# A two layer transformer on one core: attention scores in one pass from 12 bit parts, maxima 12 heads ahead, one bias on ScalarE

## The chip, the cores and the metric

The kernel runs on one core of a Trainium2 chip. The time is that of one launch on the device, in microseconds. Three runs of the kernel before took 324.24 to 324.75 us, median 324.54 us.

## The reference

Two post-norm layers over x of 8 batches, 256 tokens, width 128, all float32. The layer outputs go through residual sums and a layer norm after attention and after the feed-forward part. What matters here:

```python
# layer 0: attention with 16 heads of 8, then a feed-forward part with butterflies
qkv = x @ Wqkv + bqkv                          # q, k, v per head, d = 8
scores = einsum('bqhd,bkhd->bhqk', q, k) / sqrt(8)
out = einsum('bhqk,bkhd->bqhd', softmax(scores), v) @ Wproj + bproj
h = x @ W_exp + b_exp                          # 128 -> 512
h = gelu(butterfly(h, up_weights) + up_bias)   # linear, 9 stages of pairs
y = butterfly(h, down_weights) @ W_con + b_con + down_bias
# layer 1: low rank q, k, v, rotated q and k, 4 key heads repeated, causal mask
q = rope(x @ Wqa @ Wqb);  k, v = split(x @ Wkva @ Wkvb);  k = rope(k)
out = einsum('bhqk,bkhd->bqhd', softmax(causal(q k^T / sqrt(8))), v) @ Wout + bout
y = (silu(x @ w_gate^T) * (x @ w_up^T)) @ w_down^T     # 128 -> 384 -> 128
```

## The kernel before, in words

**Steps.** All the work is one loop over `STEPS`: g runs over the 256 heads (two layers x 8 batches x 16 heads) by `QUAD` = 4, and each engine walks the same loop with its own instructions in a hand-written order, tied by semaphores. I call the steps of a batch by g modulo 16: 0, 4, 8 and 12. An offset such as `AT_ROPE` = -36 says in which step, counted from a batch's first head, a task of that batch is done. `batch_at`, `tile_at`, `half_at`, `attention_at`, `projected_at` turn g into the batch, the 512-token tile or the half batch whose turn it is. Layer 1 begins at g = 128.

**Scores.** A head has only 8 features, so four heads share TensorE: `QK` holds each head of a group in a strip of 32 partitions, and four matmuls of different strips run beside each other. Every head's scores are made twice. `max_scores` (L382) makes them with queries on the partitions, for the row maxima, `LEAD` = 16 heads ahead of `exp_scores` (L395), which makes them with keys on the partitions, for the exponential. In the second, row 31 (`MAXROW`) of each strip holds ones against the negative row maximum, so that the subtraction comes with the product. All of it is float32. `scores` (L405) issues two heads' maxima and two heads' exponential scores in turn, twice a step, over all eight PSUM banks; the bank of a head is free again when VectorE has taken its maximum or ScalarE its exponential (`take`, L360).

**The way of a maximum.** VectorE's `maximum` (L778) writes one column of `mx` per head: a reduction in layer 0 (L789), a masked add and minimum in layer 1 (L797). After 8 heads TensorE turns `mx` (`turn_maxima`, L446, two transposes of 128 columns into 8 rows), ScalarE copies the 8 rows (`copy_maxima`, L653), and SyncE's queue moves them into the `MAXROW` rows (`maxima`, L306). This is done in steps 8 and 0 (`AT_MT`), 8 heads ahead of the use.

**The way of q and k.** TensorE projects (`project`, L455), ScalarE copies (`copy_projection`, L659), in layer 1 GpSimd rotates (L1041 to L1043, in step 12), and SyncE's queue spreads the result over `QK`, a ring of four batches (`spread`, L312).

**The rest of a step,** behind the scores on TensorE: projections, products with V (L585), transposes, and the feed-forward matmuls (L531 and L600 in layer 0, L541 and L552 in layer 1). GpSimd does the causal cut of the exponentials (L986), the layer norms (`normalise`, L938) and the preparation of layer 0's butterflies (`paths`, `mix`). VectorE adds the bias of layer 0's way up (L842); ScalarE's table for the gelu (L726) must be loaded before it and the exponential's again after it.

## Time and profile before

| | |
|---|---|
| median of the runs | 324.54 us |
| the profiled execution, its own time | 324.64 us |
| span of its instructions | 322.8 us |
| TensorE busy | 298.1 us, 92% |
| VectorE busy | 246.8 us, 76% |
| ScalarE busy | 181.5 us, 56% |
| GpSimd busy | 177.4 us, 55% |
| granted TensorE clock, mean | 0.991 |

Between the span and the execution's own time lie 1.8 us. The profile gives, per engine, busy time over the span; then groups of instructions by source line with their total and mean time; then who waited for whom. PE is TensorE, PEld its weight loads, DVE VectorE, ACT ScalarE, POOL GpSimd. A float32 matmul stands in the trace as two records, each with its own weight load. A busy share is a mean over 64 steps that have different limits, so single steps are read as well: the first exponential of each step on ScalarE marks where a step begins.

### The profile page before, as it was taken

What the parts mean: (1) busy time and instruction counts of PE and PEld (TensorE: products, weight loads), DVE (VectorE), ACT (ScalarE), POOL (GpSimd) and SP (SyncE); (2) the same over time, 40 slices, a digit from 0 to 9 for tenths busy, and PEclk for the clock granted to TensorE, in tenths of its full rate; (3) what the DMA queues carried; (4) which work ended last, traced back from release to release, by engine and by line L of the source; (5) the groups of instructions that cost most, each with busy time, mean ns of one, the idle gap of its engine ahead of it and who ended that gap; (6) DMA issues with size and microseconds to landing.
All of it is one profiled execution on the core that took longest, in us unless ns stands there. A gap on an engine that the chain in (4) does not pass through costs nothing.

```text
span 322.8 us, 10410 instructions
## 1 busy us (share of the span) xinstructions
PE 298.1 (92%) x3770; PEld 218.9 (68%) x3770; DVE 246.8 (76%) x943; ACT 181.5 (56%) x396; POOL 177.4 (55%) x296
## 2 busy tenths in 40 slices
PE   8789979999999999989999899999999999999763
PEld 4566666676677765866677657776787777767553
DVE  4887686779868697677958788597998999945555
ACT  2455665666775749456675638466555464644110
POOL 6498082321215217176266988398877746477332
PEclk9999999999999999999999999999999999999978
DMA  7743252011000110301103030301112110000000
GB/s 231 247 144 68 43 133 60 1 36 35 4 4 1 38 36 2 66 3 38 35 4 66 5 65 4 69 4 37 36 34 55 28 29 1 20 3 20 16 18 32
DMA packets 9470, 14.29 MB, mean 44 GB/s; under 512 B 2140, under 2 KB 5196, under 8 KB 9292
## 3 DMA queue, kind: packets, MB, share of 16 engines
q1 hardware_dynamic: 8988, 13.09, 16.8%
q8 instruction: 31, 0.51, 0.7%
q10 hardware_dynamic: 432, 0.53, 0.5%
q14 instruction: 19, 0.16, 0.2%
HBM read 6.28 MB, written 1.05 MB: 23 GB/s over the span
## 4 chain that ended last, share of the span: by engine, by line
PE 68%; DVE 19%; issue 6%; ACT 4%; POOL 1%; POOLq 0%; DVEq 0%; ACTq 0%
PE bank L391 17%; PE bank L585 15%; DVE mx L789 7%; PE bank L400 7%; PE bank L541 5%; PE bank L600 4%; PE bank L467 4%; PE bank L552 3%; PE bank L531 3%; DVE masked_s L797 2%; PE bank L452 2%; PE bank L563 1%; ACT E L700 1%; DVE hid L813 1%; PE bank L482 1%
## 5 line engine op out<-in xcount | busy, mean ns | idle before, releaser
L700 ACT ACTIVATE E<-bank 128x512 f32<-128x512 f32 (+1 forms) x256 | 119.3, 547 | 96.2 <-PE bank L400 95.2
L391 PE MATMUL bank<-QK 31*128 31x256 f32 (+1 forms) x1024 | 115.7, 364 | 10.1 <-DVE mx L789 4.2
L400 PE MATMUL bank<-QK 32*128 32x256 f32 (+1 forms) x1024 | 114.3, 366 | 0.9 <-ACT E L700 0.9
L391 PEld LDWEIGHTS bank<-QK 31*128 31x128 f32 x1024 | 88.3, 184 | 30.8 <-issue 11.6
L789 DVE TENSOR_REDUCE mx<-bank 128x2 f32<-128x512 f32 x128 | 79.2, 683 | 14.8 <-PE bank L391 14.7
L400 PEld LDWEIGHTS bank<-QK 32*128 32x128 f32 x1024 | 85.2, 184 | 2.7 <-ACT E L700 1.5
L797 DVE CUSTOM_DVE_ANT_0 masked_s<-bank,mask_sb 128x256 f32<-128x256 f32 (+1 forms) x256 | 73.2, 351 | 3.8 <-PE bank L391 3.5
L585 PE MATMUL bank<-E,V 128*32 128x256 f32 (+1 forms) x1024 | 55.1, 355 | 0.6 <-DVE mx L789 0.4
L986 POOL TENSOR_SCALAR_AFFINE_SELECT E<-E 128x512 f32<-128x512 f32 x64 | 39.2, 640 | 16.5 <-ACT E L700 16.5
L585 PEld LDWEIGHTS bank<-E,V 128*32 128x32 f32 x1024 | 29.3, 109 | 20.3 <-issue 2.1
L993 POOL TENSOR_TENSOR at<-turned,rec 128x256 f32<-128x256 f32 x16 | 10.1, 631 | 46.8 <-DVE rec L894 46.8
L872 DVE STREAM_TRANSPOSE turned<-bank 128x256 f32<-128x256 f32 x32 | 14.4, 450 | 22.6 <-PE bank L585 22.6
L541 PE MATMUL bank<-xt,wf 128*128 128x256 f32 x96 | 25.8, 412 | 0.2 <-DVE hid L813 0.2
L939 POOL TENSOR_SCALAR nm_a<-mv_a 128x2 f32<-128x2 f32 x15 | 2.9, 195 | 36.5 <-DVE mv_a L759 36.5
L541 PEld LDWEIGHTS bank<-xt,wf 128*128 128x128 f32 x96 | 18.3, 202 | 5.3 <-ACT E L700 2.5
L797 DVE DVE_READ_ACCUMULATOR2_ANT mx<- 128x1 f32 x256 | 21.1, 82 | 0.0
L600 PE MATMUL bank<-down,hid 128*128 128x128 f32 x128 | 16.1, 279 | 0.2 <-DVE mx L797 0.2
L600 PEld LDWEIGHTS bank<-down,hid 128*128 128x128 f32 x128 | 14.9, 192 | 1.9 <-ACT E L700 1.2
L811 DVE SCALAR_TENSOR_TENSOR gated<-th,bank 128x256 f32<-128x256 f32 x24 | 10.0, 418 | 7.8 <-ACT th L719 7.5
L719 ACT ACTIVATE th<-bank 128x256 f32<-128x256 f32 x24 | 9.3, 389 | 10.4 <-PE bank L541 9.1
L531 PE MATMUL bank<-xt,wup 128*128 128x512 f32 x32 | 15.1, 596 | 0.0
L942 POOL TENSOR_SCALAR ln_a<-r_a,nm_a,rstd_a 128x128 f32<-128x128 f32 x30 | 13.3, 452 | 1.6
(113 smaller groups left out, 400.1 us busy)
## 6 DMA issues: line engine op xcount, KB each, us to landing
QK<-qk SPq DMA_DIRECT2D x60, 64.0 KB
rs<-ry SPq DMA_DIRECT2D x16, 128.0 KB, 2.9
xb<-x_nat SPq DMA_DIRECT2D x1, 1024.0 KB, 5.0
xt<-x_t SPq DMA_DIRECT2D x1, 896.0 KB, 7.0
out<-ln_g SPq DMA_DIRECT2D x7, 128.0 KB, 1.9
wi<-wi_all SPq DMA_DIRECT2D x1, 576.0 KB, 5.1
QK<-mt SPq DMA_DIRECT2D x32, 8.0 KB
fac<-fac_u SPq DMA_DIRECT2D x1, 508.0 KB, 6.3
```

Of the source, the lines that this page charges most:

```text
L391: ins = nc.tensor.matmul(g_bank["max", m][:, cols], q, QK[rows, b % QK_RING, r, 1, keys], start=True, stop=True)
L400: ins = nc.tensor.matmul(g_bank["exp", m][:, c * T:(c + 1) * T - q0], QK[rows, b % QK_RING, r, 1, c * P:(c + 1) * P], QK[rows, b % QK_RING ...
L531: nc.tensor.matmul(bank[:, :], wup[:, c * P:(c + 1) * P], xt[:, n * FT:(n + 1) * FT], start=True, stop=True).then_inc(F0["up_ps"], 1)
L541: ins = nc.tensor.matmul(bank[:, s * T:(s + 1) * T], wf[:, s, c * P:(c + 1) * P], xt[:, i * T:(i + 1) * T], start=True, stop=True)
L585: ins = nc.tensor.matmul(bank[VCOL * j:VCOL * (j + 1), q0:T], values, E[:, (2 * n + e) % E_RING, j, k * T:(k + 1) * T - q0], start=(e == 0 ...
L600: ins = nc.tensor.matmul(bank[:, i * W:(i + 1) * W], hid0[:, c, s * P:(s + 1) * P], down[:, c, :], start=(c == 0), stop=(c == HC - 1))
L700: act.activation(E[:, a % E_RING, j, 0:n], g_bank["exp", m][:, 0:n], ACT.Exp, scale=SCALE)\
L789: ins = nc.vector.tensor_reduce(mx[:, n % 2, :, i], bank[:, :].rearrange("p (q k) -> p q k", q=QT), AX.X, ALU.max, negate=True)
L797: ins = nc.vector.tensor_tensor_reduce(out=masked_s[:, at % 2, lo:hi], in0=bank[:, lo:hi], in1=mask_sb[:, T + lo - hi:T], scale=-1.0, scal ...
L872: nc.vector.transpose(turned[:, t, :], g_bank["pv", n][:, 0:T]).then_inc(A["turned"], 1)
L942: ins = nc.gpsimd.tensor_scalar(N["ln"][:, parity, s, :], N["r"][:, s, :], N["nm"][:, s:s + 1], N["rstd"][:, s:s + 1], ALU.add, ALU.mult)
L986: nc.gpsimd.affine_select(out=e, in_=e, pattern=[[0, 4], [1, P]], compare_op=ALU.is_ge, fill=0.0, base=0, channel_multiplier=-1).then_inc( ...
```

## The change

**Parts.** q and k are each split into a high part with 12 bits of mantissa and a low part, the rest. `QK` gets the type float32r, in which a matmul is one instruction where float32 takes two. A strip of 32 rows now holds, for each of the 8 features, four products: with the rows filled by parts as high/high, high/low, low/high and low/low, one matmul over the strip sums them. The row maxima are split in the same way. Batch 0 keeps float32 (`whole`).

**More steps on the way.** ScalarE makes the high part (`high_parts`), GpSimd the low one (`low_parts`), the queue spreads both with six DMAs in place of four into `spread_qk`, and a cast to float32r writes `QK`, now a ring of two batches: by GpSimd in layer 0, by ScalarE in layer 1. The moves of `mt` and of the ones are gone.

**Maxima.** All rows of a strip are used up, so the maximum is subtracted by a matmul of its own: `less_maximum` adds ones times the two parts of the maximum into the same bank. GpSimd splits the maxima (`part_maxima`), TensorE turns them with four float32r matmuls into 128 rows, ScalarE copies 128x512 in place of 8x256. `LEAD` is 12 in place of 16, and the turning is in steps 12 and 4, four heads ahead of the use.

**Other.** ScalarE in place of VectorE adds the bias of layer 0's way up. Some tiles share room. GpSimd's `paths(0)` stands ahead of its loop with the first `part_maxima` behind it; the fetch of `xb`'s bias and the butterfly work of GpSimd are cut into smaller pieces over more steps. TensorE's start makes 12 maxima and not 16 before the loop.

The constants, and the tiles:

```diff
-ROWS, MAXROW = D, STRIP - 1
-QK_RING, V_RING, E_RING, LN_RING, BANKS = 4, 3, 4, 3, 8
+PARTS, SPREADS = 2, 6
+QK_RING, V_RING, E_RING, LN_RING, BANKS = 2, 3, 4, 3, 8
-QUAD, LEAD, AHEAD = 4, 16, 8
-AT_MT, HURRY = (-8, 0), BATCHES - 2
-AT_QK, AT_QKIN, AT_ROPE = (-44, -36), -28, -36
+QUAD, LEAD = 4, 12
+AT_MT, HURRY = (-4, 4), BATCHES - 2
+AT_QK, AT_QK1, AT_ROPE, AT_HIGH, AT_LOW, AT_SPREAD, AT_CAST = (-44, -36), -48, -36, -32, -32, -28, -16
...
-        QK = sb("QK", [P, QK_RING, GROUPS, 2, T])
+        spread_qk = sb("spread_qk", [P, GROUPS, 2, T])
+        QK = sb("QK", [P, QK_RING, GROUPS, 2, T], F32R)
+        mxp = sb("mxp", [P, 2, QT, 2, P], F32R)
+        ones_r = sb("ones_r", [P, P], F32R)
+        mt = sb("mt", [P, 2, 2, T], F32R)
```

SyncE's `spread`:

```diff
             def spread(b):
+                sp.wait_ge(A["low_ready"], b)
+                if b > 1:
+                    sp.wait_ge(A["qk_ready"], 2 * (b - 1))
+                for t in range(PARTS):
+                    sp.dma_start(spread_qk[3 * t:P:4, :, :, :], parts[:, b % 2, t, :, :]).then_inc(spread_in, 16)
+                for t in range(PARTS):
+                    for s in range(2):
+                        sp.dma_start(spread_qk[1 + t:P:4, :, s, :], parts[:, b % 2, (s + t) % 2, s, :]).then_inc(spread_in, 16)
```

TensorE: the new `less_maximum`, then in `scores` the waits and the order, then `turn_maxima`:

```diff
+            def less_maximum(m):
+                b, r, j = place(m)
+                rows = slice(STRIP * j, STRIP * (j + 1))
+                most = mt[rows, m // 8 % 2, r % 2, :]
+                if layer(b) == 0:
+                    ins = nc.tensor.matmul(g_bank["exp", m][:, :].rearrange("p (c t) -> p c t", c=2), ones_r[rows, :],
+                                           most.unsqueeze(1).broadcast_to([STRIP, 2, T]), start=False, stop=True)
+                else:
+                    for c in range(2):
+                        ins = nc.tensor.matmul(g_bank["exp", m][:, c * T:(c + 1) * T - c * P], ones_r[rows, :], most[:, c * P:T],
+                                               start=False, stop=(c == 1))
+                ins.then_inc(A["st_ps"], 1)
...
-                    elif b and m % H == 2:
-                        pe.wait_ge(qk_in[b % QK_RING], 16 * STRIPS * loads_of(b))
+                    elif b and m % 8 == 2:
+                        pe.wait_ge(A["qk_ready"], 2 * (b - 1) + m % H // 8 + 1)
...
-                        pe.wait_ge(m_in[n % 4], 16 * (n // 4 + 1))
+                        pe.wait_ge(A["mt_ready"], m // 8 + 1)
+                first = exps and exps[0] % QUAD == 2
                 for long in range(2):
+                    for m in exps if first else ():
+                        exp_scores(m, long)
                     for m in maxima:
                         max_scores(m, 1 - long)
-                    for m in exps:
+                    for m in () if first else exps:
                         exp_scores(m, long)
+                for m in exps:
+                    less_maximum(m)
...
-                pe.wait_ge(A["max_done"], 8 * (n + 1))
-                for q in range(QT):
-                    ins = nc.tensor.transpose(bank[0:8, q * P:(q + 1) * P], mx[:, n % 2, q, :], id32[:, :])
+                pe.wait_ge(A["mx_ready"], n + 1)
+                for r in range(2):
+                    for q in range(QT):
+                        ins = nc.tensor.matmul(bank[:, r * T + q * P:r * T + (q + 1) * P], mxp[:, n % 2, q, r, :], id_r[:, :], start=True, stop=True)
```

ScalarE: the copy of the maxima, `high_parts`; then in the loop the cast right after the four exponentials, the bias after the copies to `xt`, and the high parts after `copy_values`:

```diff
-                act.activation(mt[:, n % 2, :], g_bank["mt", n][0:8, 0:T], ACT.Copy).then_inc(A["mt_ready"], 1)
+                act.activation(mt[:, n % 2, :, :], g_bank["mt", n][:, :].rearrange("p (r t) -> p r t", r=2), ACT.Copy).then_inc(A["mt_ready"], 1)
...
+            def high_parts(b):
+                if layer(b) == 0:
+                    act.wait_ge(A["qk_out"], 2 * b)
+                else:
+                    act.wait_ge(A["rotated"], b - NB + 1)
+                if b > 2:
+                    act.wait_ge(A["qk_ready"], 2 * (b - 2))
+                act.activation(parts[:, b % 2, 0, :, :].bitcast(F32R), qk[:, :, :], ACT.Copy).then_inc(A["high_ready"], 1)
...
+                if (b := batch_at(g, AT_CAST, (1,))) is not None:
+                    act.wait_ge(spread_in, 16 * SPREADS * b)
+                    act.wait_ge(A["st_ps"], H * (b - QK_RING + 1))
+                    for half_batch in (slice(0, 2), slice(2, GROUPS)):
+                        act.activation(QK[:, b % QK_RING, half_batch, :, :], spread_qk[:, half_batch, :, :], ACT.Copy).then_inc(A["qk_ready"], 1)
...
+                        act.wait_ge(F0["up_ps"], HC * n + c + 1)
+                        act.activation(hid0[:, c, :], g_bank["up0", n, c][:, :], ACT.Identity, bias=bhid[:, c:c + 1]).then_inc(F0["pre_ready"], 1)
...
+                if (b := projected_at(g)) is not None and layer(b) == 0:
+                    high_parts(b)
+                if (b := batch_at(g, AT_HIGH, (1,))) is not None:
+                    high_parts(b)
```

VectorE loses:

```diff
-                        nc.vector.tensor_scalar(hid0[:, c, :], g_bank["up0", n, c][:, :], bhid[:, c:c + 1], None, ALU.add)\
-                            .then_inc(F0["pre_ready"], 1)
```

GpSimd: the new helpers, what stands ahead of the loop, the first tasks of a step, and its last:

```diff
+            def part_maxima(n):
+                pool.wait_ge(A["max_done"], 8 * (n + 1))
+                if n >= 2:
+                    pool.wait_ge(A["mt_ps"], n - 1)
+                found = mx[:, n % 2, :, :].rearrange("p q (r j) -> p q r j", r=2)
+                high, low = [mxp[:, n % 2, :, :, i:P:STRIP] for i in range(PARTS)]
+                link(nc.gpsimd.tensor_copy(high, found))
+                nc.gpsimd.tensor_tensor(low, found, high.bitcast(F32), ALU.subtract).then_inc(A["mx_ready"], 1)
+            def low_parts(b):
+                pool.wait_ge(A["high_ready"], b)
+                nc.gpsimd.tensor_tensor(parts[:, b % 2, 1, :, :], qk[:, :, :], parts[:, b % 2, 0, :, :], ALU.subtract)\
+                    .then_inc(A["low_ready"], 1)
+            low_parts(1)
+            pool.wait_ge(ld["up"], 32)
+            paths(0)
+            part_maxima(0)
             for g in STEPS:
+                if (n := half_at(g, AT_MT)):
+                    part_maxima(n)
+                if (b := batch_at(g, AT_CAST, (0,))) is not None and b:
+                    for half_batch in (slice(0, 2), slice(2, GROUPS)):
+                        nc.gpsimd.tensor_copy(QK[:, b % QK_RING, half_batch, :, :], spread_qk[:, half_batch, :, :]).then_inc(A["qk_ready"], 1)
...
+                if (b := batch_at(g, AT_LOW)) is not None and b > 1:
+                    low_parts(b)
```

## Rows read from the trace of the kernel before

**Rows 1.** The page: busy time (share of the span) and instructions.
```profile
PE 298.1 (92%) x3770; PEld 218.9 (68%) x3770; DVE 246.8 (76%) x943; ACT 181.5 (56%) x396; POOL 177.4 (55%) x296
```

**Rows 2.** Waits: who waited for what, us in total, times, longest.
```profile
ACT E L700 <- PE bank L400: 95.2, 60, 3.7
```

**Rows 3.** Busy time in stretches: steps 64 to 92, then steps 64, 76, 84, 92.
```profile
core 0: us, PE busy (x) PEld busy (x) DVE busy (x) ACT busy (x) POOL busy (x), PEclk, DMA share, GB/s
89.91:127.63 37.72, 37.18 (x472) 25.84 (x468) 29.41 (x65) 24.76 (x48) 14.74 (x25) 1.00 0.08 17
89.91:94.08 4.17, 4.17 (x60) 3.41 (x56) 1.77 (x7) 2.29 (x6) 0.38 (x1) 1.00 0.01 2
103.06:106.95 3.89, 3.89 (x48) 2.96 (x44) 2.49 (x5) 3.55 (x9) 1.97 (x5) 1.00 0.01 2
111.48:116.20 4.72, 4.72 (x44) 2.78 (x40) 4.29 (x8) 2.56 (x6) 2.36 (x3) 1.00 0.18 41
120.75:127.63 6.88, 6.53 (x106) 3.98 (x102) 5.36 (x12) 6.82 (x9) 5.73 (x8) 1.00 0.01 2
```

**Rows 4.** The same for layer 1: steps 144, 148 and 192, 196.
```profile
181.39:184.72 3.33, 2.36 (x44) 1.76 (x41) 2.31 (x17) 2.12 (x6) 3.25 (x3) 1.00 0.01 2
184.72:190.52 5.80, 5.80 (x80) 3.74 (x76) 4.60 (x21) 2.24 (x6) 4.69 (x8) 1.00 0.46 81
235.20:239.56 4.36, 4.36 (x58) 3.71 (x55) 4.16 (x23) 2.24 (x7) 3.16 (x7) 1.00 0.06 17
239.56:243.85 4.29, 4.29 (x78) 3.20 (x74) 3.32 (x22) 2.51 (x6) 3.15 (x7) 1.00 0.46 86
```

**Rows 5.** Timeline of PE: start us, us from first start to last end, instruction.
```profile
82.11 0.38 PE L391 MATMUL bank<-QK 31*128 31x256 f32 x2
82.33 0.38 PE L391 MATMUL bank<-QK 31*128 31x256 f32 x2
...
247.68 0.27 PE L391 MATMUL bank<-QK 31*128 31x128 f32 x2
...
247.79 0.28 PE L391 MATMUL bank<-QK 31*128 31x128 f32 x2
...
104.72 0.60 PE L522 MATMUL bank<-id,ln_f 128*128 128x128 f32 x4
```

**Rows 6.** Groups of ACT: line, instruction, count | busy us, mean ns.
```profile
L657 ACT ACTIVATE mt<-bank 8x256 f32<-8x256 f32 x32 | 11.4, 358 | 1.8 <-PE bank L452 1.8
L726 ACT ACTIVATE hid<-hid 128x2048 f32<-128x2048 f32 x4 | 7.6, 1910 | 0.0
L672 ACT ACTIVATE ry<-bank 128x512 f32<-128x512 f32 x8 | 4.8, 605 | 0.5 <-PE bank L467 0.2
```

**Rows 7.** Groups of POOL.
```profile
L1043 POOL TENSOR_TENSOR qk<-ry,rs 128x512 f32<-128x512 f32 x8 | 10.2, 1281 | 0.6
L977 POOL MEMSET QK<- 128x2048 f32 x3 | 5.3, 1806 | 0.0
L955 POOL TENSOR_TENSOR path<-fac 128x16 f32<-128x16 f32 x2 | 0.4, 219 | 5.6 <-DMA u_sb<-u 5.6
```

**Rows 8.** Groups of DVE.
```profile
L789 DVE TENSOR_REDUCE mx<-bank 128x2 f32<-128x512 f32 x128 | 79.2, 683 | 14.8 <-PE bank L391 14.7
L842 DVE TENSOR_SCALAR hid<-bank,bhid 128x512 f32<-128x512 f32 x16 | 11.8, 749 | 2.2 <-PE bank L531 1.8
```

**Rows 9.** Timeline of the first 24 us: POOL's paths, the first exponentials.
```profile
15.61 3.06 POOL L955 TENSOR_TENSOR path<-path,fac 128x32 f32<-128x32 f32 x5
...
20.09 2.28 ACT L700 ACTIVATE E<-bank 128x512 f32<-128x512 f32 x4 [1.42 <-PE bank L400]
```

**Rows 10.** Timeline of ACT in layer 1: four exponentials of a step, one tanh.
```profile
237.29 0.38 ACT L719 ACTIVATE th<-bank 128x256 f32<-128x256 f32 x1 [0.23 <-PE bank L541]
239.56 1.64 ACT L700 ACTIVATE E<-bank 128x384 f32<-128x384 f32 x4 [1.88 <-PE bank L400]
```

More of the change, by code:

```diff
@@ L183, in block_kernel, with part @@
         other = sb("other", [P, HC, W + 1])
-        facs = [sb(f"fac{i}", [P, HC, FAC]) for i in range(2)]
-        path = [sb(f"path{i}", [P, HC, FAC]) for i in range(2)]
+        room_a, room_c = sb("room_a", [P, 2 * GROUPS * T]), sb("room_c", [P, 4 * HC * FAC])
+        def part(room, first, shape):
+            size = int(np.prod(shape))
+            names = "abcd"[:len(shape)]
+            return room[:, first:first + size].rearrange(f"p ({' '.join(names)}) -> p {' '.join(names)}", **dict(zip(names, shape)))
+        facs = [part(room_c, i * HC * FAC, [HC, FAC]) for i in range(2)]
+        path = [part(room_c, (2 + i) * HC * FAC, [HC, FAC]) for i in range(2)]
         bfw_sb = sb("bfw_sb", [P, 2, 2, 2, HC])
@@ L390, in max_scores @@
                     cols, keys = (slice(T, T + P), slice(0, P)) if c == 0 else (slice(0, T), slice(0, T))
[L391 removed]
+                ins = nc.tensor.matmul(g_bank["max", m][:, cols], both[:, 0, c * P:(c + 1) * P], both[:, 1, keys], start=True, stop=True)
                 if c == 0:
```

213 lines of the change are left out of this document (95 added, 118 removed).

## The prediction

> **What bounds the kernel now.** I read the busy table first: TensorE is busy for 298.1 us, 92% of the span, and no other engine passes 76% [rows 1]. The waits agree: ScalarE's largest idle time, 95.2 us, ended with exponential scores from TensorE [rows 2]. Then I read single steps. From step 64 to 92, one 512-token tile of layer 0, the eight steps take 37.72 us, TensorE is busy in 37.18, VectorE in 29.41, ScalarE in 24.76, GpSimd in 14.74 [rows 3]. So TensorE bounds layer 0. Only step 92 stands apart: ScalarE is busy in 6.82 of 6.88 us there, by the gelu between two table loads. In layer 1 TensorE fills steps 148, 192 and 196, but VectorE has 4.16 of 4.36 us in step 192 [rows 4]. What TensorE gives up there, VectorE takes over after a few tenths of a us.
>
> **Scores, what goes.** Float32 records of one strip are 0.22 us apart for 256 columns and 0.11 us for 128, and a matmul is two records, so 0.43 us [rows 5]. A step of layer 0 has 16 matmuls on four strips: four rounds, 1.72 us.
>
> **Scores, what comes.** No float32r matmul is in this trace. One instruction of 256 columns is bounded below by the 0.11 us of a 128-column record, which pushes the same number of column passes (two for each column, if the four products of a float32 matmul are shared evenly by its two records), and above by the 0.22 us of one 256-column record. I take 0.11, since the second pass of such a record has no counterpart when one part is multiplied by one part. The added `less_maximum` is 512 columns for each head, and issue is in order: exponential and maximum scores for two rounds, `less_maximum` of two strips for two rounds, the first of them beside the exponential scores of the other two strips, and so on. I count seven rounds a step, 0.77 us (1.54 at the upper price). Saved: 0.95 us a step in layer 0. In layer 1 the rounds before are 768 columns of four passes, 1.3 us; after, the two short `less_maximum` matmuls of a head follow each other and I count about 1.0 us. Saved: 0.3 us.
>
> The Trainium skill, FP8 and Floating Point Precision, section TensorE Precision Notes, says that true FP32 is four passes and that a reduced mode reads 4 bytes and truncates to FP22. By it one pass of 256 columns is a quarter of 0.43 us, again 0.11; the trace agrees on the four passes only as far as two records of 0.22 us go.
>
> **The turn of the maxima.** Two transposes, 0.11 us apart like the four of L522 [rows 5], become four matmuls of 128 columns: +0.22 us on TensorE in steps 4 and 12. ScalarE's copy goes from 8x256 in 0.36 us to 128x512, as L672 in 0.60 us [rows 6]: +0.25 us. The matmul could cost up to 0.22 us each, as bound above.
>
> **ScalarE.** L672 and L726 (512 columns 0.60, 2048 columns 1.91 us) give 0.85 ns a column [rows 6]. Added are: the high part, 0.6 us a batch; the bias, 16 times about 0.6 us where VectorE took 0.75 [rows 8]; in layer 1 the cast, two of 1024 columns, 1.04 us each. In steps 64 to 92 this makes 24.76 + 4 x 0.25 + 2 x 0.6 + 4 x 0.6 = 29.4 us.
>
> **VectorE** loses 11.8 us of biases [rows 8], 3.0 in each of the four tiles: 29.41 becomes 26.4 in that stretch.
>
> **GpSimd.** Low part: 512 columns with two inputs, as L1043, 1.28 us a batch. Split of the maxima: two small operations as the 128x16 one of 0.22 us, with a wait between, 0.55 us twice a batch. The cast in layer 0, 2 x 1024 columns, lies between 0.9 us each (half a memset of 2048) and 2.6 (twice L1043); one input is nearer to the memset, I take 1.2 each [rows 7]. Layer 0: +4.8 us a batch on 7.4, no bound. Layer 1: +2.4 us.
>
> **The sum, layer 0.** No engine is near the old 37.7 us now, so I take for each step the latest of: TensorE's time less 0.95 (plus 0.22 in steps 4 and 12); ScalarE's with its additions; VectorE's; and the loop of four exponentials (2.29 us, step 64) and the scores behind them (0.7 to 0.8), 3.1 us. In the order of the tile: step 64 3.1 (was 4.17), then 3.5 and 4.0; step 76 3.5 (3.89; ScalarE's additions of 0.85 to its 3.55 partly sink into the lighter next step); 3.7; step 84 4.2 (4.72, two biases and a high part), 3.8; step 92 7.2, for the gelu's 6.82 remain and the larger copy of maxima joins. Sum 33.0, against 37.7: -4.7 us a tile. Two and a half such tiles from step 32 to 108 give -12 us; steps 4 to 28 have no gelu, less TensorE work and batch 0 in float32: -2. Together -14 us.
>
> **The start.** The first exponential runs at 20.09 us [rows 9]. Before it now stand 12 maxima and not 16, 4 x 0.62 us less (79.2 us over 128 [rows 8]), but the first split of the maxima stands behind GpSimd's `paths(0)`, whose end was at 15.3 us (its twin began at 15.61 [rows 9]); then split 0.55, turn 0.6, copy 0.6, scores 1.3: about 19. -1 us.
>
> **The sum, layer 1: a new chain.** This is where I expect a loss. Count from the first exponential of a step 0, S. ScalarE runs four exponentials, 1.64 [rows 10]; two casts, 2.08; the copy `ry`, moved here from step 4, 0.60; a tanh, 0.38 [rows 10]; the high part, 0.60: with gaps S + 5.5. GpSimd's last task of that step, `low_parts`, waits for it: S + 6.8. Queued behind that wait is step 4's `part_maxima`: S + 7.4. TensorE waits for it before `turn_maxima`, and behind that stands the rest of its step 4. That rest, for step 196, is 4.29 less 1.6 of scores with their drain less 0.86 of a projection that moves: 1.85 us [rows 4]. So the scores of step 8 end their first head at S + 7.4 + 0.5 + 1.85 + 0.6 = S + 10.35. Before, steps 192 and 196 took 4.36 + 4.29 = 8.65: +1.7. For steps 144 and 148 the rest is 5.80 - 2.46 = 3.3, the end S + 11.8 against 9.13: +2.7. The same sum over all seven such pairs (steps 112 to 208) gives +17 us. Given back: TensorE is shorter by 0.3 in each of steps 8 and 12, and VectorE and GpSimd use the pause to clear what they would have done in step 8: together I take 1.1 us a batch, 7.7 us. Net +9.5 us. From step 224 on no low part is left: -1 us.
>
> Total: 324.6 - 14 - 1 + 9.5 - 1 = 318 us, on the profiled execution's own time; the median is 0.1 us below it.
>
> **DMAs and other edits** I put at nothing. Two moves of the maxima and four of q and k become six, issued within one step; they are due 12 heads after their issue, three steps or 11 us. If that cover failed, the cast would wait and with it, in layer 1, ScalarE's exponentials. The maxima's 8 KB moves leave the path, and their slack of a step with them. Ring 2 in place of 4 asks only that the exponentials of batch b - 2 are issued; they are, a step earlier. Smaller pieces of `mix` lie beside TensorE.
>
> **Rivals.**
> A (forecast): as above, 311 to 324 us, chance 0.48.
> B: the chain does not bind, because ScalarE reaches the high part while TensorE is still in step 4's scores. For: ScalarE is busy in 2.24 of 4.36 us in step 192 [rows 4]. Against: its added 3.3 us fill just that. Time 318 - 9.5 = 308.5; range 303 to 311; 0.20.
> C: one float32r pass has the upper price, 0.22 us per 256 columns. Layer 0 then saves 0.18 us a step and loses 0.22 in two of four, nothing in sum; layer 1 pays 1900 columns, 1.6 us, for 1.3, 32 x 0.3 = +9. With the chain: 324.6 - 1 + 9.5 + 8 = about 341; 0.13. For: a transpose of 128 columns, a single record, is no faster than the two-pass records beside it (0.11 us, [rows 5]). Against: its weight load alone may set that.
> D, slower: GpSimd becomes the bound of layer 1. It has 3.2 us in each of steps 192 and 196 and over 4.6 in step 148 [rows 4]; with +2.4 us a batch it holds about 15.6 us of work in 16.9, and every wait of its queue (high part, variance, reciprocals) comes on top. It decides from the point where these waits pass 1.3 us a batch; at 3 us of them a batch takes 18.6, +1.7 us more than before for seven batches and hardly less for the pairs with layer norms of layer 0: +20 in layer 1 in place of +8.5, about 329; 0.17.
> That float32r does not run as one pass at all (0.43 us a round, seven rounds for four) would cost 1.3 us a step in layer 0 alone, over 360 us; 0.02.
>
> The Trainium skill, TensorE: Matmul & The Clock Gate, section LDWEIGHTS, gives a weight load as its columns over 1.2 GHz, 107 ns for 128 columns, and lets loads overlap only with matmuls of other row groups or into the background buffer. By it, if the load did not overlap its own strip, a round would be 0.21 us, C's price.
>
> **How the numbers follow.** 318 us is A's. The range, 303 to 334, takes in A, B and D with their bounds and leaves out C and the last, 15 in 100, and a little of the tails. This kernel's measurement can tell 0.2%, 0.65 us, from no change. Faster: 0.44 of A, all of B, a little of D: 0.65. Same 0.05. Slower 0.30.
>
> **What would show it.** Scores: the group of L391's successor with one record per matmul, 512 columns' `less_maximum` beside it, and rounds 0.11 us apart; 0.22 would be C. Layer 0: 33 us from step 64 to 92 and TensorE busy below 95%. Chain: in layer 1 TensorE's wait before `turn_maxima` in step 4 put down to GpSimd, 2 to 3 us, seven times, with `low_parts` just before; missing, it is B. GpSimd over 90% busy from step 128 on without a wait for ScalarE would be D. I am wrong if step 92's kind is longer than 7.5 us, for then ScalarE's additions do not sink anywhere.

## The result, and the profile after

The changed kernel takes 359.5 us (median of 4 executions, 355.0 to 363.8) against 324.6 us of the kernel before, run beside it on the same chip: ratio 1.094, interval 1.091 to 1.097. The forecast was 318 us, the range 303 to 334. It was wrong in sign and by 41.5 us. Medians are of all executions; ratios, and what is called a short mean below, take only those within 1.5% of a kernel's shortest, since the others had TensorE's lower clock for longer. The short mean of the changed kernel, over its four such executions here and in `after_again`, is 354.9 us.

The profiled execution of after is one of its longer ones (span 362.0 us; its shorter spans are 353.3 and 353.5), so stretches are read from it to find where time goes, and the ratio says how much.

The page of after, busy time, and the row of TensorE's granted clock in 40 slices (tenths of 2.4 GHz), first of before, then of after:

```profile
PEclk9999999999999999999999999999999999999978
```
```profile
PE 304.8 (84%) x3258; PEld 217.0 (60%) x3258; DVE 233.0 (64%) x927; ACT 223.4 (62%) x444; POOL 219.2 (61%) x391
...
PEclk9759996999999999969998699697699969899988
```

TensorE has 512 instructions fewer and yet more busy time than in [rows 1], and no engine is busy for the whole span. The clock row says half of why: before has the lower of the two clocks (1.2 in place of 2.4 GHz) for 5.8 us, all in its last 13 us; after has it for 71.6 us, in eleven stretches (its two shorter executions, by their mean granted clocks of 0.923 and 0.928, for 54 and 51 us). Matmuls in those stretches last up to twice as long. The waits say the other half (who waited for what; us in total, times, longest):

```profile
POOL parts L1026 <- ACT parts L697: 36.1, 10, 11.1
...
PE bank L467 <- POOL mxp L1021: 15.9, 10, 2.9
```

This is the chain that the prediction drew: GpSimd's `low_parts` (L1026) waits for ScalarE's high part (L697), and TensorE's turn of the maxima (L467) waits for GpSimd's split (L1021), ten times. Cut by the first exponentials of the steps, the 39 us between the two profiled spans lie as follows (us against before; combine is the last but two of the experiments):

| stretch | forecast | after | combine |
|---|---|---|---|
| up to the first exponential | -1 | +4.3 | -0.7 |
| steps 0 to 28 | -2 | +5.2 | +2.9 |
| steps 32 to 108 | -12 | -4.1 | -6.7 |
| steps 112 to 220, with all seven pairs of the chain | +9.5 | +30.7 | +0.8 |
| the rest | -1 | +3.1 | +0.8 |
| sum | -6.5 | +39.2 | -2.9 |

Some 7 us in the first two rows belong to this execution of after: in `swap_first`, which differs only in the order of two tasks on SyncE and whose start ran at the upper clock, they are -0.4 and +2.8. Layer 0 gave a third of its 12 us, and the stretch of the chain cost three times its 9.5. Steps 112 to 220 of before, after and combine:

```profile
145.37:268.39 123.02, 118.83 (x1625) 89.47 (x1622) 102.05 (x570) 73.35 (x166) 85.81 (x135) 1.00 0.16 33
...
150.77:304.52 153.75, 126.35 (x1416) 92.85 (x1412) 95.13 (x549) 98.72 (x195) 101.78 (x172) 0.87 0.19 62
...
140.88:264.70 123.82, 111.73 (x1416) 84.82 (x1408) 94.94 (x549) 97.77 (x194) 101.83 (x172) 0.97 0.24 76
```

The columns are those of [rows 3]: the span, then busy time of TensorE, its weight loads, VectorE, ScalarE and GpSimd. After and combine issue the same 1416 matmuls of TensorE there. Of the 29.9 us between them, 14.6 are the same matmuls taking longer (the lower clock has 41 us of this stretch in after, 7 in combine) and 15.3 are TensorE waiting.

Two steps of layer 1 and the tile of steps 64 to 92 of after, as [rows 3] and [rows 4] (busy us of each engine, granted clock):

```profile
core 0: us, PE busy (x) PEld busy (x) DVE busy (x) ACT busy (x) POOL busy (x), PEclk, DMA share, GB/s
195.34:199.99 4.65, 2.70 (x36) 2.07 (x35) 3.27 (x24) 4.65 (x9) 3.43 (x4) 1.00 0.01 4
...
199.99:209.68 9.69, 7.99 (x68) 4.21 (x64) 1.73 (x10) 3.64 (x9) 4.72 (x8) 0.65 0.38 127
...
109.61:114.32 4.71, 4.14 (x44) 3.30 (x46) 3.49 (x9) 4.54 (x10) 3.99 (x8) 1.00 0.00 0
...
126.50:133.87 7.37, 6.83 (x90) 4.30 (x94) 5.78 (x13) 7.31 (x10) 6.37 (x9) 1.00 0.03 7
97.49:133.87 36.38, 33.28 (x368) 22.18 (x368) 26.48 (x60) 28.86 (x53) 21.43 (x38) 1.00 0.20 67
```

Step 144 is full on ScalarE (4.65 of 4.65). Step 148 takes 9.69 us where [rows 4] has 5.80, at a mean clock of 0.65. The tile of layer 0 takes 36.38 us, not 33.0.

The timeline of step 148 in after shows both losses one after the other (start us, us, instruction, idle time before it and what ended it):

```profile
199.47 0.67 ACT L697 ACTIVATE parts<-qk 128x512 fp32r<-128x512 f32 x1
...
200.22 1.27 POOL L1026 TENSOR_TENSOR parts<-qk,parts 128x512 f32<-128x512 f32 x1 [1.37 <-ACT parts L697]
...
201.44 0.21 POOL L1020 CAST mxp<-mx 128x16 fp32r<-128x16 f32 x1
...
201.73 0.24 POOL L1021 TENSOR_TENSOR mxp<-mx,mxp 128x16 fp32r<-128x16 f32 x1
...
202.12 1.09 PE L467 MATMUL bank<-id_r,mxp 128*128 128x128 f32 x4 [1.68 <-POOL mxp L1021]
...
203.00 3.72 PE L545 MATMUL bank<-xt,wup 128*128 128x512 f32 x4
...
206.65 2.38 PE L599 MATMUL bank<-E,V 128*32 128x256 f32 x32
...
210.27 1.98 PE L545 MATMUL bank<-xt,wup 128*128 128x512 f32 x4
```

High part, low part, split, turn: TensorE waits 1.68 us. Then the same four matmuls of L545 that take 1.98 us in the next step at 2.4 GHz take 3.72 at 1.2. Here the clock costs more than the wait it came with: the clock fell at 201.7 us, inside the wait.

### The profile page after: what moved, and what is told of

Same layout as the page of the kernel before. It is cut to its first block, busy times and chain, and to the rows that moved or that the text cites. A ratio compares the mean times of both kernels' runs of the same rounds, so it can differ in the third digit from the quotient of the medians.

```text
span 362.0 us, 9594 instructions
## 1 busy us (share of the span) xinstructions
PE 304.8 (84%) x3258; PEld 217.0 (60%) x3258; DVE 233.0 (64%) x927; ACT 223.4 (62%) x444; POOL 219.2 (61%) x391
## 4 chain that ended last, share of the span: by engine, by line
PE 45%; POOL 27%; issue 11%; DVE 9%; ACT 3%; SPq 2%; DMA 1%; POOLq 0%; DVEq 0%; ACTq 0%
PE bank L599 11%; PE bank L545 4%; PE bank L467 4%; PE bank L387 4%; PE bank L555 4%; POOL parts L1026 3%; POOL E L1050 3%; PE bank L397 3%; PE bank L614 3%; POOL qk L1106 2%; PE bank L484 2%; POOL room_c L1104 2%; POOL room_c L1105 2%; DVE mx L832 2%; PE bank L566 2%
## 5 line engine op out<-in xcount | busy, mean ns | idle before, releaser
L840 DVE CUSTOM_DVE_ANT_0 room_c<-bank,mask_sb 128x256 f32<-128x256 f32 (+1 forms) x256 | 72.9, 349 | 7.5 <-PE bank L387 7.5
L397 PE MATMUL bank<-QK 32*128 32x256 f32 x480 | 56.1, 316 | 14.8 <-DVE hid L856 4.5
L599 PE MATMUL bank<-E,V 128*32 128x256 f32 (+1 forms) x1024 | 64.1, 399 | 0.1
L387 PE MATMUL bank<-QK 32*128 32x256 f32 x480 | 57.2, 315 | 6.0 <-ACT QK L733 2.4
L397 PEld LDWEIGHTS bank<-QK 32*128 32x128 f32 x480 | 37.1, 189 | 25.4 <-issue 15.2
L387 PEld LDWEIGHTS bank<-QK 32*128 32x128 f32 x480 | 37.5, 189 | 22.1 <-issue 12.6
L1050 POOL TENSOR_SCALAR_AFFINE_SELECT E<-E 128x512 f32<-128x512 f32 x64 | 39.2, 639 | 4.4 <-ACT E L726 4.4
L1026 POOL TENSOR_TENSOR parts<-qk,parts 128x512 f32<-128x512 f32 x15 | 19.1, 1275 | 36.1 <-ACT parts L697 36.1
L467 PE MATMUL bank<-id_r,mxp 128*128 128x128 f32 x128 | 24.1, 317 | 19.8 <-POOL mxp L1021 15.9
L467 PEld LDWEIGHTS bank<-id_r,mxp 128*128 128x128 f32 x128 | 19.5, 219 | 26.8 <-DVE mx L832 10.2
L671 ACT ACTIVATE mt<-bank 128x512 fp32r<-128x512 f32 x32 | 19.6, 612 | 15.4 <-PE bank L467 15.4
L406 PE MATMUL bank<-mt,ones_r 32*128 32x512 f32 x128 | 27.9, 425 | 0.0
L410 PE MATMUL bank<-mt,ones_r 32*128 32x256 f32 (+1 forms) x256 | 25.3, 281 | 0.0
```

Of the source, the lines that this page charges most:

```text
L387: ins = nc.tensor.matmul(g_bank["max", m][:, cols], both[:, 0, c * P:(c + 1) * P], both[:, 1, keys], start=True, stop=True)
L397: nc.tensor.matmul(g_bank["exp", m][:, c * T:(c + 1) * T - q0], both[:, 1, c * P:(c + 1) * P], both[:, 0, q0:T], start=(c == 0), stop=False)
L406: ins = nc.tensor.matmul(g_bank["exp", m][:, :].rearrange("p (c t) -> p c t", c=2), ones_r[rows, :], most.unsqueeze(1).broadcast_to([STRIP ...
L410: ins = nc.tensor.matmul(g_bank["exp", m][:, c * T:(c + 1) * T - c * P], ones_r[rows, :], most[:, c * P:T], start=False, stop=(c == 1))
L467: ins = nc.tensor.matmul(bank[:, r * T + q * P:r * T + (q + 1) * P], mxp[:, n % 2, q, r, :], id_r[:, :], start=True, stop=True)
L599: ins = nc.tensor.matmul(bank[VCOL * j:VCOL * (j + 1), q0:T], values, E[:, (2 * n + e) % E_RING, j, k * T:(k + 1) * T - q0], start=(e == 0 ...
```

## The experiments

All are single cores of the same kind, each beside the kernel before. Unless said otherwise the base is the changed kernel, and every edit moves work, none changes what is computed.

**Is it the bias, or the run?** The changed kernel once more, as it is.

> The changed kernel as it is, for a second profile beside the others and for its spread. Theory (the clock follows the waits, and where it falls differs between launches): the time lies again between 355 and 364 us, and the first exponential comes at about 19 us where the clock is up in the first 25 us and at about 24 where it is not.

358.9 us (353.1 to 364.4), ratio 1.088 [1.076, 1.100]: two executions of one kernel differ by up to 11 us, which calls for caution with differences of a few us below. The kernel before, run beside each group, has short means of 324.9 to 326.2 us. Then ScalarE's four additions of the bias a tile (L752) given back to VectorE:

```
-    act.activation(hid0[:, c, :], bank, ACT.Identity, bias=bhid[:, c:c + 1])
+    nc.vector.tensor_scalar(hid0[:, c, :], bank, bhid[:, c:c + 1], None, ALU.add)
```

> The changed kernel with the bias of layer 0's way up back on VectorE. Theory 1: ScalarE has 11 us of work less in steps 20 and 24 of each tile; ScalarE, not VectorE, decides step 20 (5.09 of 5.25 us at step 52), so 1 us a tile comes back, and the wait chain of layer 1 is untouched except in steps 116 to 152: 350 to 355 us. Rival (VectorE is the next bound): 3 us a tile are lost, 365.

359.7 us, ratio 1.104 [1.095, 1.112], short mean 358.6. The interval touches that of after, so no gain or cost of the second part is shown; if anything it gives a little (steps 32 to 124 take 2.0 us more in this profile than in that of after). All of the loss is the scores' part.

**The chain in layer 1.** `low_parts` one step later in layer 1, so that step 4's split of the maxima doesn't stand behind it:

```
-    if (b := batch_at(g, AT_LOW)) is not None and b > 1:
+    if (b := batch_at(g, AT_LOW, (0,))) is not None and b > 1:
+        low_parts(b)
+    if (b := batch_at(g, AT_LOW + QUAD, (1,))) is not None:
         low_parts(b)
```

> The changed kernel with layer 1's low parts made one step later, behind the split of the maxima of step 4, so that this split no longer queues behind a wait for ScalarE. Theory 1 (chain, then clock): TensorE waited 2 to 3 us before the turn of the maxima in step 4 of batches 7 to 14, and each such wait was followed by a stretch at the lower clock in which its work took twice as long; without the chain both go, steps 4 of layer 1 fall from 7 to 10 us to about 5, the time from 355 to about 328 us, and the granted clock from 0.92 to about 0.96. Rival (thin matmuls): the clock falls because single-pass scores leave TensorE less work to show, whatever waits there are; then the clock stays near 0.93 and the time falls by no more than 8 to 10 us, to 345.

355.8 us median (356.9, 356.9, 354.7 and once 345.7, too uneven for an interval): far less than the theory wanted. Step 148 falls from 9.69 to 5.09 us, as it said, but steps 208 and 212 take 7.5 and 8.5 (4.2 and 9.9 in after). The trace names what came in place of the wait:

```profile
POOL room_c L1104 <- DMA room_c<-room_c: 18.2, 6, 7.0
```

and its timeline:

```profile
195.87 0.67 ACT L697 ACTIVATE parts<-qk 128x512 fp32r<-128x512 f32 x1
...
197.36 1.28 POOL L1026 TENSOR_TENSOR parts<-qk,parts 128x512 f32<-128x512 f32 x1
...
199.95 2.56 SPq L322 DMA_DIRECT2D spread_qk<-parts  x4
...
202.61 5.83 SPq L339 DMA_DIRECT2D room_c<-room_c  x8
...
209.87 1.27 POOL L1104 TENSOR_TENSOR room_c<-room_c,ropec_sb 128x512 f32<-128x512 f32 x1 [4.20 <-DMA room_c<-room_c]
```

SyncE issues the spread of batch b (L319, L322), which waits for `low_parts` of b, and behind it the eight DMAs that swap halves for the rotation of the next batch (L339). The rotation (L1104) makes the q and k whose high part lets `low_parts` run. So low part, spread, swap, rotation, high part and again low part are one loop through an in-order queue. The swap itself had grown:

```profile
187.93 1.16 SPq L343 DMA_DIRECT2D rs<-ry  x2
```
```profile
201.52 1.23 SPq L319 DMA_DIRECT2D spread_qk<-parts  x2
202.79 2.56 SPq L322 DMA_DIRECT2D spread_qk<-parts  x4
205.45 5.00 SPq L339 DMA_DIRECT2D room_c<-room_c  x8
```

The first line is before, the others after: two DMAs in 1.16 us became eight in 5.00, some 0.6 us each, and with the spread SyncE spends 8.8 us in a row. The prediction put "DMAs and other edits" at nothing, and its list of moves leaves these eight out.

**The order on SyncE.** Only the swap ahead of the spread in SyncE's step:

```
-    if (b := batch_at(g, AT_SPREAD)) is not None and b >= 2:
-        spread(b)
     ... the swap of the same step ...
+    if (b := batch_at(g, AT_SPREAD)) is not None and b >= 2:
+        spread(b)
```

> The changed kernel with one edit on SyncE's queue: in a step that has both, the eight moves of the rotation's halves are issued ahead of the six moves that spread q and k. Theory 2 (a loop through the queue): in layer 1 low part, spread, swap, rotation, high part and low part again follow each other once a batch, since the eight small moves (5 us of issue) stand in the queue behind a spread that waits for the low part. With the swap ahead, the rotation starts some 5 us sooner in batches 12 to 14, GpSimd's rotation no longer waits for a DMA, step 212 falls from 9.9 to about 7.5 us, and the time by 4 to 8 us, to about 349. If only the place of the low part on GpSimd mattered (theory 1), nothing changes: 355.

351.1 us, 1.079 [1.070, 1.087], short mean 350.9. TensorE still waits for the split nine times, 12.5 us in all. Both edits together:

> Both orders mended: the low parts of layer 1 behind the split of the maxima on GpSimd, and the swap ahead of the spread on SyncE's queue. Theory 2: the two together are what the first edit alone could not do; GpSimd waits neither for ScalarE nor for a DMA for more than 1 us, steps 4 of layer 1 take about 5 us (6 to 7 where TensorE's other work is long), and the time falls to about 330 us with a clock of 0.95 or more. Rival (GpSimd full): its work of 15.6 us a batch and the waits in it keep layer 1 at 18 us a batch, about 340 us.

339.0 us, 1.040 [1.032, 1.048], short mean 338.8. Against 354.9 the two give 16 us together. Apart, the swap gave 4, and the low part 9 in its one short execution and less in the other three: each alone leaves the loop closed at the other place, as the two traces show. The wait of L467 for L1021 falls from 15.9 to 3.4 us (three times), that of L1104 for the swap is gone, and the lower clock covers 41 us (51 to 54 in the shorter executions of after).

**What the clock takes.** Can a wait alone do this to the kernel before? In it GpSimd clears a scratch tile (four linked operations of 525 ns and a small one) after the first exponential of seven steps (116, 132 to 212), and TensorE waits for that between its scores and the rest of the step. (The kernel before has no turn of the maxima in these steps; the wait stands where the changed kernel has it.) All of the kernel's work stays, nothing is in float32r:

```
+    if g in PAUSES:
+        pe.wait_ge(pause, PAUSES.index(g) + 1)
...
+    if g in PAUSES:
+        pool.wait_ge(A["exp_done"], g + 1)
+        for _ in range(4):
+            link(nc.gpsimd.memset(slow[:, :], 0.0))
+        nc.gpsimd.memset(slow[:, 0:1], 0.0).then_inc(pause, 1)
```

> The kernel before, with a made wait: in step 4 of batches 7 to 13 TensorE waits, between its scores and the rest of the step, for four fills of 512 columns and one of 1 on GpSimd that start after the step's first exponential. No float32r matmul, no other edit. If the clock falls after waits, whatever the matmuls: seven waits of 2 to 3 us, about 15 us of them, are followed by stretches at the lower clock and the time rises by 20 to 28 us, to about 348, with a mean clock near 0.95. If the lower clock belongs to the single-pass scores, it stays at 0.99 and only the waits themselves are paid, 10 to 16 us: about 338.

355.0 us, 1.088 [1.080, 1.097]. The trace (busy time, waits, then step 148's first matmuls):

```profile
PE 312.0 (88%) x3770; PEld 225.4 (64%) x3770; DVE 246.6 (70%) x943; ACT 181.7 (51%) x396; POOL 192.5 (54%) x331
```
```profile
PE bank L470 <- POOL slow L989: 15.3, 6, 3.5
...
PE bank L521 <- POOL slow L989: 2.5, 1, 2.5
```
```profile
197.95 2.07 PE L470 MATMUL bank<-xt,wl 128*128 128x256 f32 x4 [3.48 <-POOL slow L989]
199.82 3.06 PE L536 MATMUL bank<-xt,wup 128*128 128x512 f32 x4
```

The kernel is 29 us longer by its median, and this profile is 31.7 us longer than that of before. The seven waits are 17.8 us of it, and that is all that TensorE's idle time grew by (from 24.7 to 42.5 us, the span less its busy time). The other 13.9 us are the same 3770 instructions being busy for 312.0 in place of 298.1 us: not GpSimd's added work, nor another wait, but slower matmuls. The lower clock covers 36.3 us against 5.8, so each of the 30.5 us more at 1.2 GHz cost 0.46 us (an estimate from these numbers; the same sum for steps 112 to 220 of after and combine gives 14.6 over 34, 0.43). This kernel has no float32r matmul, so the lower clock needs none. It came within or right behind each of the seven waits, of 2.1 to 3.5 us.

Then the other way: in the changed kernel, idle matmuls of 128 columns on a bank that is claimed anyway, six ahead of the turn of odd half batches from 15 on and three ahead of the first scores that wait for new keys in layer 1.

```
+    if n % 2 and n >= 15:
+        fill(bank, 6)
     pe.wait_ge(A["mx_ready"], n + 1)
```

> The changed kernel, with matmuls of no use put where TensorE waits: six of 128 columns before the wait of the turn in step 4 of batches 7 to 15 (1.3 us at the full clock, under a wait of 1.7 us and more) and three before the wait for the cast keys of layer 1. The chain stays as it is. Theory 1: the clock stays up in layer 1, mean 0.96 or more; the chain's waits remain; the time falls by what the lower clock cost there, some 15 to 20 us, to about 338. Rival (GpSimd or ScalarE bound alone, the clock a mere companion): the time stays within 3 us of 355 or rises.

347.5 us, 1.067 [1.060, 1.074], short mean 346.7: 78 more matmuls (156 records), 8 us less time than 354.9; the lower clock covers 17 to 26 us in its shorter executions, 51 to 54 in those of after. The idle matmuls compute nothing and bring no input earlier, so these 8 us were the clock's. With `low_parts` late as well:

> Both edits together. Theory 1: with the chain gone the fillers before the turn find little to fill and cost about as much as they save: 325 to 332 us, clock 0.97. If the two causes were independent, the gains of the two single runs would add up in full and the time would be below 315.

353.3 us, 1.083 [1.073, 1.093], against 355.8 without the idle matmuls. The spans overlap; with the loop through SyncE open nothing more can be said. The same for the start, where some profiles have the lower clock from 14 to 28 us and the first exponential at 22 to 24 us, others (order_both's too) the upper clock and 19.3: on the base of order_both, idle matmuls ahead of the first maxima and exponentials,

> The same, and at the start matmuls of no use where TensorE waits for VectorE's maxima and for the first copy of the maxima (19 of 128 columns in all). Theory (the clock of the start): the clock was low from 13.9 to 27.6 us because TensorE waited for VectorE; filled, it stays up, the first exponential comes at about 20 us and not at 24.4, and 4 us are gained on the run without this edit. Rival: the start is bound by VectorE's maxima and GpSimd's paths whatever the clock; gain under 1 us.

342.0 us, a loss on 339.0: the clock was up at the start as in order_both's profile, and the first exponential ran at 24.4 us in place of 19.3, since the idle matmuls took 4.9 us themselves. With both kinds of idle matmuls, three ahead of each turn:

> The same, and fillers in layer 1 as well: three before the turn in step 4 of batches 7 to 15, three before the wait for the cast keys. If waits are left that let the clock fall in layer 1, 3 to 6 us are gained on the run without them and the clock is 0.98; if none are left, the fillers cost up to 0.6 us a batch, 4 us. Either way above 324 us if the claims of banks behind VectorE's maxima, which cost TensorE about 1 us a step in layer 0, bound the rest.

341.3 us. Idle matmuls pay only where TensorE waits anyway, and after the reordering there was little of that left.

**What else the change puts on the path.** On the base of order_both, ScalarE's second half of the cast one step later, from step 0 to step 4, where it has room:

```
-    if (b := batch_at(g, AT_CAST, (1,))) is not None:
-        for half_batch in (slice(0, 2), slice(2, GROUPS)):
+    for late, half_batch in enumerate((slice(0, 2), slice(2, GROUPS))):
+        if (b := batch_at(g, AT_CAST + QUAD * late, (1,))) is not None:
```

> The kernel with both orders mended, and layer 1's cast of the second half of a batch moved from step 0 to step 4 of ScalarE. Theory 3: with the chain gone, ScalarE bounds steps 0 of layer 1 (busy for 4.65 of 4.65 us in three of them) and has 1 us to spare in the steps 4; seven steps get 0.5 to 0.9 us shorter, 3 to 6 us in all: about 334 us. If VectorE and GpSimd bound the batch as a whole, nothing changes: 339.

330.2 us (10 executions, 325.1 to 335.5), 1.002 [0.996, 1.008], short mean 327.1. That is 8.8 us by the medians and 11.8 by the short means, the largest effect of one edit. The batch of steps 192 to 204 (first order_both, then this kernel; layout as above):

```profile
242.63:259.84 17.21, 15.45 (x210) 12.62 (x210) 14.80 (x86) 12.22 (x28) 15.00 (x28) 1.00 0.27 86
```
```profile
237.50:253.87 16.37, 15.34 (x210) 12.52 (x210) 14.90 (x86) 12.30 (x28) 15.24 (x29) 1.00 0.29 91
```

0.8 us a batch is the share where the clock stayed up; the rest is mostly steps 164, 212 and 228, at 8.5, 7.4 and 6.7 us before the edit and 7.1, 4.4 and 4.4 after it, where waits and the lower clock went together. The two profiles are 10.5 us apart, and 7.5 of them are TensorE busy for less time (284.9 for 292.4 us) with the same 3258 instructions.

For layer 0 the trace of after shows TensorE waiting for VectorE's scans of the maxima before it may take a bank:

```profile
101.56 0.66 PE L467 MATMUL bank<-id_r,mxp 128*128 128x128 f32 x4 [0.68 <-DVE mx L832]
...
106.34 0.71 PE L577 MATMUL bank<-wproj_sb,att 128*128 128x128 f32 x4 [0.76 <-DVE mx L832]
```

The scores come in a shorter burst, VectorE still needs 0.68 us for each pair of maxima, and the next bank in the old order is one that it has not read. On the base of order_both, layer 1's order in layer 0 too:

```
-    i = ((0, 2, 3, 1) if g < NB * H else (2, 3, 0, 1))[i]
+    i = (2, 3, 0, 1)[i]
```

> The kernel with both orders mended, and in layer 0 the first two tasks behind the scores claim the banks of the exponential scores and not first one of VectorE's maxima. Theory 4: since the scores take 1 us less, the first claim comes before VectorE has read its first bank, and TensorE hands back about 0.7 us in many steps of layer 0 (waits before L467 and L577 put down to VectorE's maxima); with the other banks 4 to 8 us come back: about 333 us. If ScalarE reads its banks just as late, no change: 339.

336.5 us, 1.030 [1.021, 1.038], short mean 336.3: 2.5 us, within the intervals. The tile of steps 64 to 92 shows the effect without the scatter:

```profile
97.80:133.10 35.30, 33.05 (x374) 21.94 (x376) 26.08 (x60) 28.72 (x52) 21.05 (x36) 1.00 0.21 68
```

35.30 us against 36.38: 1.1 us where those two waits are 1.4 (step 80, though, grew from 4.3 to 4.6).

**All of it together.** The two edits on SyncE and GpSimd, the cast in two steps and the order of claims:

> cast_split and claims in one kernel: swap ahead of spread, low parts and half of the cast one step later in layer 1, and claims in the order 2, 3, 0, 1 in layer 0 too. If the two savings are of separate stretches (layer 1's steps of kind 0, and the steps of layer 0 that wait for a free bank), they add: 330.2 less the 2.5 us between order_both and claims, about 327.5 us, and the tile of steps 64 to 92 takes 35.3 us with step 28 still at 7.9. If one only moved the wait into the other's stretch, it stays at 330.

325.5 us (4 executions, 321.7 to 332.5), 0.997 [0.990, 1.003], short mean 324.2: the savings add (338.8 less 11.8 and 2.5 is 324.5), and the kernel is level with before. The page of its shortest execution, and steps 192 to 220:

```profile
PE 281.6 (88%) x3258; PEld 204.2 (64%) x3258; DVE 232.9 (73%) x927; ACT 221.9 (69%) x444; POOL 218.6 (68%) x391
...
PEclk9999996999999999999998799999999999999979
```
```profile
232.41:264.70 32.29, 29.89 (x412) 24.35 (x412) 29.75 (x170) 24.13 (x53) 27.52 (x53) 1.00 0.25 84
```

The same 3258 matmuls that kept TensorE busy for 304.8 us do so for 281.6, 16.5 us less than before: this is what the change takes from TensorE once the clock is up (17 us at 1.2 GHz are left). In steps 192 to 220 VectorE, with 29.75 us, is as busy as TensorE.

One stretch was still open, step 28 (7.3 us here, 8.8 in after, 4.75 before), where in after the turn waited for a split behind GpSimd's `mix` of weights:

```profile
53.97 1.29 POOL L1006 TENSOR_TENSOR up<-own,other 128x516 f32<-128x516 f32 x1
...
56.20 1.09 PE L467 MATMUL bank<-id_r,mxp 128*128 128x128 f32 x4 [2.26 <-POOL mxp L1021]
```

combine with that `mix` a step later:

```
-    if g == BXD + 2 * QUAD:
+    if g == BXD + 3 * QUAD:
```

> combine with GpSimd's last mix of the composition of weights (617, 617 and 1283 ns ahead of the split of the maxima of step 32) put behind the work of the next step. Theory that step 28's 7.9 us are this queue: the split comes some 2.5 us earlier, step 28 falls to about 5.3 us and the kernel to about 325 us; the later weights are wanted only from step 36. Rival, that step 28 waits for something else as well (GpSimd has 7.2 us of work in it): the step falls by less than 1 us and the time stays at combine's.

324.6 us (6 executions), 0.994 [0.989, 0.999], short mean 323.4. Step 28 only fell to 7.0 us: TensorE is busy for 6.8 of them at 1.2 GHz, and the lower clock began at 47.2 us, before the step. The queue of `mix` was not what made the step long in these kernels; why the clock falls at 47 us was not found. The ratio, just under 1, is the best of all; its interval ends at 0.999, so "slightly faster than before, if at all" is all it carries. With idle matmuls in it (three and three):

> combine_mix with 3 idle matmuls of 128 columns ahead of the turn of the odd half batches from 15 on, and 3 ahead of the scores that wait for the cast keys in layer 1. Theory that part of what is left is matmuls at 1.2 GHz after waits: the lower clock shrinks from some 20 us to under 10 and the time falls by 2 to 4 us. Rival, that with the waits mostly gone the idle matmuls only cost their 0.35 us at 15 or so places: 1 to 5 us longer.

328.4 us, 1.010 [1.003, 1.016], lower clock 14 to 27 us over its executions: no gain, most waits to fill are gone.

## Why the prediction was wrong, step by step

**The price of one pass: right; what a step's scores cost: too low.** The successors of L391 have one record a matmul. The scores of one step of combine (layer 0):

```profile
96.79 0.38 PE L387 MATMUL bank<-QK 32*128 32x256 f32 x2
...
97.02 0.28 PE L387 MATMUL bank<-QK 32*128 32x256 f32 x2
...
97.14 0.39 PE L406 MATMUL bank<-mt,ones_r 32*128 32x512 f32 x2
97.38 0.39 PE L397 MATMUL bank<-QK 32*128 32x256 f32 x2
...
97.60 0.28 PE L397 MATMUL bank<-QK 32*128 32x256 f32 x2
...
97.72 0.39 PE L406 MATMUL bank<-mt,ones_r 32*128 32x512 f32 x2
```

0.12 us from the second round to the third is the 0.11 that was taken, and rival C is out. But the first round of a burst takes 0.23 us: it carries its own weight load, and the strip's second load starts only 0.11 us after the first. With two bursts and 512 columns at the end of each a step's scores take 1.15 us, not 0.77: 0.6 us are saved a step, not 0.95. The Trainium skill (TensorE: Matmul & The Clock Gate, LDWEIGHTS) gives a 128-column load 107 ns; the loads of a strip start 0.11 us apart here, which agrees. Of the two ways of overlap that it allows, beside matmuls of other row groups or into the background buffer, the second would fit what is seen: after the first round a strip's loads run beside the strip's own matmul, and a round is 0.12, not 0.21.

**The sum of layer 0, -4.7 us a tile: measured -1.3, and -2.4 with other claims.** Over steps 32 to 108 the forecast's 12 us were 4.1. Steps 64, 84 and 88 came close to the drawing (3.1, 4.0, 3.9 for 3.1, 4.2, 3.8). Steps 68, 72 and 80 took 4.4, 4.7 and 4.3 for 3.5, 4.0 and 3.7, and claims put the first two at 4.1 and 4.0. The failed step is to take for each step "the latest of" the engines' busy sums: it left out that a shorter burst of scores makes TensorE claim banks that VectorE has not read yet, 1.1 us of the 3.4 that are missing. Step 76 is ScalarE's, 4.71 us for a forecast 3.5, with ScalarE busy for 4.54, so its additions did not "sink into the lighter next step"; that is another 1.2. The rest, step 80 above all, is open. In steps 0 to 28 the forecast -2 was +2.4 to +2.9 where the start ran at the upper clock, all of it step 28 (7.8 us for 4.75 in `swap_first`), whose cause stays open. Step 92 took 7.37 us for 7.2, below the 7.5 that was named as the sign.

**The start: right where the clock is up, helped by a rounding.** The terms that the prediction adds for it make 18.4 us, written as about 19. The first exponential runs at 19.3 us in order_both and combine (forecast 19), at 24.4 in after's profile, with the lower clock from 13.9 to 27.6.

**The sum of layer 1: the chain seen rightly, and its price of +9.5 us the step that failed most, against +30.7.** Seven of the ten waits for the split are in the steps 4 that were named, with `low_parts` in front (in step 116 an addition of 1.3 us, L1115, as well): 2.7, 1.8, 1.7, 1.8, 0.8, 0.5 and 2.9 us, 12.1 in all (the other three are in steps 4, 28 and 140). Rival B is out, and the waits are not longer than was forecast (the sum was 17 less 7.7, 9.3 us, written as 9.5). Two things were missing beside them. First, the DMAs "at nothing": their completion was weighed (11 us of cover), but not the swap's growth from two to eight, nor SyncE's own issue time for them, 5.0 us, nor that the swap stands behind a wait of the spread. Untying both places is worth 16 us. Second, a wait was taken to cost its length. Pauses of 17.8 us made the profiled kernel before 31.7 longer, idle matmuls gave back 8 in the kernel after, and of the 29.9 us between after and combine in steps 112 to 220 the slower matmuls are 14.6. After step 220, where 1 us was to be gained, step 228 takes 6.7 us for 3.6: TensorE waits 1.6 us for a sum of VectorE (L887), and the clock is down for half of the step.

**ScalarE's step 0.** Counted (S + 5.5), but only as one link of the chain. It is also a bound of its own: step 144 has 4.65 us of ScalarE in 4.65. Moving half the cast gave 9 to 12 us, though most of that through the clock.

**Rival D** did not come by its sign, GpSimd over 90% busy: it is busy for 66% of steps 112 to 220 in after, and for 82% in combine, where the stretch takes hardly longer than before. But D's condition, waits in GpSimd's queue of over 1.3 us a batch, was met: of the 36.1 us that L1026 waited for high parts, 19.0 are two waits before 30 us, but 15.1 are six waits from step 116 on, over 2 us a batch. A and D looked at one queue from two sides, and neither priced what came of it.

The sign of the forecast hung on layer 0's 14 us; combine shows what they were with the waits out: 6.7 us over steps 32 to 108 and less than nothing up to step 28. By short means the 31 us from after to combine_mix fall to the edits, in this order only, so: 16 for the queues, 12 for the cast, 3 for the claims, 1 for the `mix`, the last two within the scatter.

## What to carry to other kernels

A pass that gets cheaper on the bounding engine pays only if its inputs, made now by other engines (high part, low part, split, cast), do not stand in in-order queues ahead of what that engine waits for next: write out each queue, the DMA issuer's too, with the wait at its head, and look for loops through two of them. Price DMAs by the issuer's time per instruction as well as by their landing. And where TensorE is the bounding engine and was hardly idle before, price new waits of 2 to 3 us at 1.6 to 1.8 times their length (29 and 31.7 us for 17.8 in pause_before), until a profile shows the granted clock staying up.

## What the runs showed of the hardware that was not expected

- The granted clock fell from 2.4 to 1.2 GHz beside single waits of only 1.4 to 3.5 us in kernels that were busy on TensorE at over 80% (after and pause_before). Not every such wait does it: in after, 1.76 us in step 132 left the clock up. Float32r scores do not lower it by themselves: in after the clock stayed up from 61.7 to 157.3 us, and fell inside the first wait of TensorE over 0.8 us after that start, the 2.7 us of step 116.
- SyncE needs some 0.6 us to issue one DMA (two in 1.16 us, eight in 5.00), and everything behind it in its queue waits for that.
- Executions of one kernel differ by 9 to 11 us (after 355.0 to 363.8, combine 321.7 to 332.5), before by 6 (323.5 to 329.9 in eleven beside combine): where and how often the clock falls differs from one execution to the next.
- A copy to float32r of 128x1024 took 1077 ns on ScalarE and 1039 ns on GpSimd. For ScalarE that is what the float32 copies of [rows 6] give for 1024 columns (0.60 us for 512 and 1.91 for 2048, so an estimated 1.04):

```profile
L733 ACT ACTIVATE QK<-spread_qk 128x1024 fp32r<-128x1024 f32 x16 | 16.2, 1077 | 0.0
...
L1043 POOL CAST QK<-spread_qk 128x1024 fp32r<-128x1024 f32 x14 | 14.2, 1039 | 0.5 <-DMA spread_qk<-parts 0.5
```
